# Two fp32 products made from split operands, with new engine orders and the first depthwise tap on ScalarE

## The reference, cut to what matters

```
x = x + L0(_gn(x))     # gate: sparsemax(mean(x) @ gate_w.T + gate_b); weight = sum_k gate_k * expert_w[k]; 1x1 convolution
x = x + L1(_gn(x))     # depthwise 3x3, BN, relu, prune(4.0); pointwise 256x256, BN, relu, prune(0.001)
x = x + L2(_gn(x))     # q, k, v; q2n, k2n normalised squares; kv = k2n^T v; attn = v + q2n kv / sqrt(N); @ Wln + bln
x = x + L3(_gn(x))     # 3x3 box filter
```

## Time and profile before

| what | value |
|---|---|
| times of three runs | 1614.42, 1614.85, 1618.74 us; median 1614.85 |
| the profiled execution | 1618.37 us, span 1616.7 us |
| PE busy | 1517.5 us (94%) |
| DVE busy | 1308.9 us (81%) |
| ACT busy | 1186.3 us (73%) |
| POOL busy | 295.7 us (18%) |

### The profile page before, as it was taken

How to read it: one execution, slowest core, us unless ns; L and a number is a source line. 1 busy time by engine, 2 the same in 40 slices (tenths; PEclk the granted TensorE clock), 3 DMA queues, 4 the chain that set the end, 5 groups by cost and what they waited for, 6 DMA issues and landing times.

```text
span 1616.7 us, 27652 instructions
## 1 busy us (share of the span) xinstructions
PE 1517.5 (94%) x9282; PEld 1219.5 (75%) x9282; DVE 1308.9 (81%) x2355; ACT 1186.3 (73%) x2440; POOL 295.7 (18%) x232
## 2 busy tenths in 40 slices
PE   4369999999999999999999999999999999999983
PEld 2147878788778788887877888878787887787773
DVE  4758788888888888988888889888888888887436
ACT  3356778877777887777778877777788777776752
POOL 1100022222112122221221222212222221121100
PEclk9679999999999999999999999999999999999986
DMA  4100144333344433334444333344443333344431
GB/s 133 37 20 24 38 100 91 70 83 89 89 79 99 99 75 84 79 82 97 79 99 99 66 88 85 79 82 97 99 90 69 84 87 88 60 81 80 80 61 40
DMA packets 45572, 127.88 MB, mean 79 GB/s; under 512 B 3793, under 2 KB 4817, under 8 KB 45522
## 3 DMA queue, kind: packets, MB, share of 16 engines
q0 software_dynamic: 24480, 72.26, 27.4%
q1 hardware_dynamic: 20946, 54.98, 8.9%
q10 hardware_dynamic: 96, 0.00, 0.0%
HBM read 29.29 MB, written 97.94 MB: 79 GB/s over the span
## 4 chain that ended last, share of the span: by engine, by line
PE 89%; DVE 6%; ACT 3%; issue 2%; DMA 0%; ACTq 0%; DVEq 0%
PE conv_ps L477 35%; PE tile_ps L630 12%; PE tile_ps L559 10%; PE conv_ps L618 9%; PE small_ps L605 4%; PE tile_ps L504 4%; PE tile_ps L491 3%; PE tile_ps L587 3%; PE tile_ps L526 3%; PE tile_ps L523 2%; PE tile_ps L556 2%; DVE h L823 2%; PE tile_ps L575 1%; PE small_ps L468 1%; PE small_ps L461 1%
## 5 line engine op out<-in xcount | busy, mean ns | idle before, releaser
L823 DVE SCALAR_TENSOR_TENSOR h<-xpad,dw_sb,h 128x784 f32<-128x784 f32 x512 | 492.4, 1028 | 0.0
L630 PE MATMUL tile_ps<-k,xT 112*128 112x256 f32 x896 | 201.4, 383 | 0.0
L630 PEld LDWEIGHTS tile_ps<-k,xT 112*128 112x128 f32 x896 | 171.6, 192 | 22.4
L1325 POOL TENSOR_SCALAR pw_masked<-pw_sb,hmask 128x256 f32<-128x256 f32 x64 | 117.3, 1840 | 385.7 <-DVE hmask L831 377.3
L559 PE MATMUL tile_ps<-wqk,xn_parts 128*112 128x256 f32 x1344 | 187.6, 294 | 0.0
L1315 POOL DMA_DIRECT2D out<-row_sums x90 | 108.4, 1204 | 429.4 <-DMA out<-row_sums 384.3
L1036 ACT ACTIVATE junk<-x 128x784 bf16<-128x784 f32 x192 | 162.9, 852 | 27.2 <-DVE x L850 17.9
L477 PE MATMUL conv_ps<-h,pw_masked 128*128 128x392 f32 x512 | 176.7, 499 | 5.5 <-issue 5.5
L618 PE MATMUL conv_ps<-x,mixed 128*128 128x392 f32 (+1 forms) x512 | 174.5, 493 | 2.2 <-ACT mixed L1075 1.1
L559 PEld LDWEIGHTS tile_ps<-wqk,xn_parts 128*112 128x112 f32 x1344 | 169.6, 175 | 0.1
L477 PE MATMUL conv_ps<-xn_parts,w_out 128*128 128x392 f32 x768 | 150.9, 345 | 0.0
(11 more groups left out here) (146 smaller groups left out, 2722.5 us busy)
## 6 DMA issues: line engine op xcount, KB each, us to landing
out<-row_sums POOLq DMA_DIRECT2D x90, 784.0 KB, 7.1
x<-x SPq DMA_DIRECT2D x32, 784.0 KB, 5.4
out<-x SPq DMA_DIRECT2D x30, 784.0 KB, 3.4
expert_sb<-expert_rows SPq DMA_DIRECT2D x8, 256.0 KB, 5.1
out<-x SPq DMA_DIRECT2D x4, 392.0 KB, 2.4
x<-w_qk SPq DMA_DIRECT2D x1, 512.0 KB
x<-w_vT SPq DMA_DIRECT2D x1, 256.0 KB
x<-w_ln SPq DMA_DIRECT2D x1, 256.0 KB
```

Of the source, the lines that this page charges most:

```text
L630: mm = nc.tensor.matmul(tile_ps[:, KX_BANK, i * C:(i + 1) * C], xT[:, m, half(i)], k2[:, m, :], start=(m == 0), stop=(m == M - 1))
L823: ins = nc.vector.scalar_tensor_tensor(acc, view, scalar, acc, ALU.mult, ALU.add)
L1325: nc.gpsimd.tensor_scalar(pw_masked[:, j, :], pw_sb[:, j, :], hmask[:, j:j + 1], 0.0, ALU.mult, ALU.add).then_inc(pw_masked_ready.sem, 1)
```

## The change

Both fp32 products take the form that the others have. The pointwise weight is split once in setup. The prune mask is applied to the activation, not to the weight: ACT makes the high part (`h_high`, scale = mask) and DVE the low part (`h_low`). For the mixed convolution ACT makes the high part of x0, in the instruction that also sums x0 (`x0_high`). POOL makes the low part (`x0_low`), ACT the high part of the mixed weight, and DVE its low part (`mixed_low`). POOL's `mask_weights` is gone, and ACT makes the first depthwise tap of each half. The orders on all four engines change. `h_parts` and `q_parts` share one tile.

```diff
@@ pe
             def pointwise(C_, halves):
-                pe.wait_ge(h_ready.sem, h_ready.at(C_))
-                pe.wait_ge(pw_masked_ready.sem, pw_masked_ready.at(C_))
+                pe.wait_ge(h_lo.sem, h_lo.at(C_))
...
-                    conv_tile(j, [(pw_masked[:, i, :], h[:, C_.odd, i, :]) for i in range(J)]).then_inc(pw_mm.sem, 1)
+                    conv_tile(j, by_parts(pw_parts, h_parts)).then_inc(pw_mm.sem, 1)
@@ pe, mixed_conv
-                pe.wait_ge(mixed_ready.sem, mixed_ready.at(A))
+                pe.wait_ge(mean_low.sem, mean_low.at(A))
+                pe.wait_ge(x0_lo.sem, x0_lo.at(A))
+                pe.wait_ge(mixed_lo.sem, mixed_lo.at(A))
...
+                    for n, (u, v) in enumerate(((0, 0), (0, 1), (1, 0))):
+                        for i in range(J):
+                            for a in range(2):
+                                width = HALF + 2 * a
+                                mm = nc.tensor.matmul(conv_ps[:, 2 * j + a, 0:width],
+                                                      mixed_parts[:, u, i * C + j * P:i * C + (j + 1) * P],
+                                                      x0_parts[:, v, i, a * HALF:a * HALF + width],
...
@@ pe, step
                     key_norms(E)
+                if A.active:
+                    gate_logits(A)
+                if E.active:
                     attention_weights(E)
                     value_out(B, D, E, F, 1)
-                if A.active:
-                    gate_logits(A)
@@ dve
+            def h_low(C_):
+                for j in range(J):
+                    dve.wait_ge(h_hi.sem, h_hi.at(C_, j + 1))
+                    nc.vector.scalar_tensor_tensor(h_parts[:, 1, j, :], h[:, C_.odd, j, :], hmask[:, j:j + 1],
+                                                   h_parts[:, 0, j, :].bitcast(F32), ALU.mult,
+                                                   ALU.subtract).then_inc(h_lo.sem, 1)
+            def mixed_low(A):
+                dve.wait_ge(mixed_hi.sem, mixed_hi.at(A))
...
+                    nc.vector.scalar_tensor_tensor(mixed_parts[:, 1, cols], small_ps[:, cols], gn_r[:, 0, i:i + 1],
+                                                   mixed_parts[:, 0, cols].bitcast(F32), ALU.mult,
...
@@ dve, setup
+                parts_of(pw_parts, pw_raw)
@@ dve, step
                 if E.active:
+                    q_low(E)
                     key_norms(E)
-                    q_low(E)
-                if B.active:
-                    depthwise(B, slice(0, 1))
+                if A.active:
+                    sparsemax(A)
+                    mean_lows(A)
                 if E.active:
                     attention_weights_low(E)
-                if A.active:
-                    sparsemax(A)
                 if t.first:
                     setup_weights()
                 if D.active:
                     x2_low(D)
                 if E.active:
-                    make_x3(E)
-                if B.active:
-                    depthwise(B, slice(1, 3))
+                    make_x3(E, 0)
                 if C_.active:
                     h_mask(C_)
+                if E.active:
+                    make_x3(E, 1)
...
+                if C_.active:
+                    h_low(C_)
+                if A.active:
+                    mixed_low(A)
+                if B.active:
+                    depthwise(B, slice(0, 2))      # 16 taps now: 2, then 9, then 5 (were 1, 2, 9 and 6 of 18)
@@ act
+            def x0_high(Z):
+                act.wait_ge(x_loaded.of(Z), x_loaded.at(Z))
+                if (Z - 1).active:
+                    act.wait_ge(conv0_mm.sem, conv0_mm.at(Z - 1))
+                for j in range(J):
+                    nc.scalar.activation(x0_parts[:, 0, j, 0:HW], x0[:, Z.odd, j, :], ACT.Identity,
+                                         accum_out=gn_in[:, 0, j:j + 1]).then_inc(x0_hi.sem, 1)
+            def first_tap(B, j):
...
+                nc.scalar.activation(image_rows(h[:, B.odd, j, :]), xpad[:, j, 0:H, 0:W], ACT.Identity,
+                                     scale=dw_sb[:, j, 0:1]).then_inc(dw_step[j].sem, 1)
@@ act, step
                 if D.active:
                     normalise_x2(A, D)
+                if C_.active:
+                    relu_h(C_, 0)
+                    relu_h(C_, 1)
                 if E.active:
                     attention_weights_high(E)
-                if C_.active:
-                    relu_h(C_, 0)
+                if F.active:
+                    normalise_x3(F)
                 if D.active:
                     x2_high(D)
-                if F.active:
-                    normalise_x3(F)
                 if C_.active:
                     sum_over_h(C_, 0)
-                    relu_h(C_, 1)
+                    sum_over_h(C_, 1)
+                    h_high(C_)
                 if A.active:
                     scaled_mix(A)
-                if C_.active:
-                    sum_over_h(C_, 1)
+                if B.active:
+                    for j in range(J):
+                        first_tap(B, j)
...
                     fourth_powers(D)
+                if Z.active:
+                    x0_high(Z)
@@ pool
-            def normalise_x1(A, B, C_):
+            def normalise_x1(A, B, C_, E):
                 pool.wait_ge(gn.sem, gn.at(A))
+                if E.active:
+                    pool.wait_ge(x3_ready.sem, x3_ready.at(E, 1))
...
+            def x0_low(Z):
+                for j in range(J):
+                    pool.wait_ge(x0_hi.sem, x0_hi.at(Z, j + 1))
+                    nc.gpsimd.tensor_tensor(x0_parts[:, 1, j, 0:HW], x0[:, Z.odd, j, :], x0_parts[:, 0, j, 0:HW].bitcast(F32),
+                                            ALU.subtract).then_inc(x0_lo.sem, 1)
@@ pool, step
                 if F.active and not F.in_tail:
-                    add_rows(F)
+                    add_rows(F, range(2))
+                if Z.active:
+                    x0_low(Z)
+                if F.active and not F.in_tail:
+                    add_rows(F, range(2, BOX_ROWS))
```

More of the change, by code:

```diff
@@ L163, in build @@
         h = sb("h", [P, 2, J, HW])
-        pw_masked = sb("pw_masked", [P, J, C])
         x2 = sb("x2", [P, 2, J, HW])
@@ L248, in build @@
         gn = sig("gn", GN_DONE)
-        gn_sums = [sig(f"gn_sums{n}", 2 * J if n == 0 else J) for n in range(4)]
+        gn_sums = [sig(f"gn_sums{n}", J) for n in range(4)]
         gn_mm = sig("gn_mm")
@@ L351, in build @@
         PAIRS = [[2 * b, 2 * b + 1] if 2 * b + 1 < M else [2 * b] for b in range(4)]
-        TAP_TURNS = [(j, n) for n in range(TAPS) for j in range(J)]
+        TAP_TURNS = [(j, n) for n in range(1, TAPS) for j in range(J)]
         block = ctx.enter_context(nc.Block())
@@ L842, in make_x2, with mean_lows @@
                                                    accum_out=gn_in[:, 2, j:j + 1]).then_inc(x2_ready.sem, 1)
+            def mean_lows(A):
+                dve.wait_ge(mean_column.sem, mean_column.at(A))
+                nc.vector.tensor_tensor(x0_parts[:, 1, :, HW:XW], gn_avg[:, 0, 0:2].unsqueeze(2).to_broadcast([P, J, 2]),
+                                        x0_parts[:, 0, :, HW:XW].bitcast(F32), ALU.subtract).then_inc(mean_low.sem, 1)
+            def mixed_low(A):
+                dve.wait_ge(mixed_hi.sem, mixed_hi.at(A))
+                for i in range(J):
+                    cols = slice(i * C, (i + 1) * C)
+                    nc.vector.scalar_tensor_tensor(mixed_parts[:, 1, cols], small_ps[:, cols], gn_r[:, 0, i:i + 1],
+                                                   mixed_parts[:, 0, cols].bitcast(F32), ALU.mult,
+                                                   ALU.subtract).then_inc(mixed_lo.sem, 1)
             def make_x1(A):
@@ L850, in make_x1, with make_x3 @@
                     nc.vector.scalar_tensor_tensor(split(x1[:, A.odd, j, :]), conv_banks(j), shift,
-                                                   split(x0[:, A.odd, j, 0:HW]), ALU.subtract, ALU.add,
+                                                   split(x0[:, A.odd, j, :]), ALU.subtract, ALU.add,
                                                    accum_out=gn_in[:, 1, j:j + 1]).then_inc(x1_ready.sem, 1)
-            def make_x3(E):
-                if (E - 1).active and not (E - 1).in_tail:
-                    dve.wait_ge(stored.of(E - 1), stored.at(E - 1))
-                for j in range(J):
-                    if (E - 1).active:
-                        dve.wait_ge(x3pad_ready.sem, x3pad_ready.at(E - 1, j + 1))
-                    dve.wait_ge(attn_mm.sem, attn_mm.at(E, j + 1))
-                    nc.vector.scalar_tensor_tensor(split(x3_of(E)[:, j, :]), conv_banks(j), b_out[:, j:j + 1],
-                                                   split(x2[:, E.odd, j, :]), ALU.add, ALU.add,
-                                                   accum_out=gn_in[:, 3, j:j + 1]).then_inc(x3_ready.sem, 1)
+            def make_x3(E, j):
+                if (E - 1).active:
```

(23 more changed lines are left out.)

141 lines of the change are left out of this document (73 added, 68 removed).

## The result

The changed kernel takes 1596.88 us (median of 4 runs, 1595.6 to 1599.65); the kernel before, run beside it, 1615.56. The ratio is 0.9884, 95% interval 0.9864 to 0.9904: faster, by 1.2%. The forecast was 1597. The profiled execution has a span of 1596.0 (before 1616.7), 20.7 less.

The account below looks back on a forecast made before the run. PE was taken as the bound, busy 46.44 of 46.44 us a full round. 28 full rounds x (46.45 - 45.5) = 26.6, less 7.2 for filling and draining, is 19.4 saved: 1597 us, 8-in-10 range 1577 to 1624.

Parts of the forecast that it names:

- round 0: Filling: mixed product waits for DVE's mixed_low behind the longer setup; round closes at 49.2 instead of 39.6, +9.6 us.
- round 1: Filling: all taps wait behind the mixed weight on DVE, +4.8 us.
- round 2: Filling: the pointwise product starts earlier, no longer waiting for POOL and taps, -4.8 us.
- The front: Start of a full round: relus on ACT and sparsemax on DVE precede attention's parts; ACT makes PE wait 0.9 us.
- The products: PE's pointwise and mixed products in split form save 0.97 and 0.89; PE's work falls from 46.44 to 44.58 a round.
- The new form is not cheaper here: Rival: split products save little, for instance through the 394 columns; a round of 46.2, 1615 us, chance 0.03.
- DVE's round: DVE's work, waits and POOL's blocks: 41.5 + 1.7 = 43.2 occupied; with remaining waits 45.5, equal to PE's.
- the thin place: DVE's round equals PE's 45.5, so each us of DVE lateness costs about half a us a round.
- Filling and draining: First rounds and drain together cost +7.2 us, with bounds of +2 and +14.
- Everything hides: Rival: ACT's high part comes sooner, PE keeps 1.6 or more of its 1.86; round 44.8, 1576 us, chance 0.12.
- The lock bites harder: Rival: POOL's x0_low or xpad blocks DVE more, DVE 1.2 later; round 46.1, 1612 us, chance 0.18.
- DVE becomes the bound: Rival: x0_low or its blocks make DVE late, PE waits 1.9; round 46.5, 1625 us, slower, chance 0.17.

Follow-up runs that it names:

- the doubled low part: Changed kernel, but GpSimd makes the low part of x0 twice in every half, two more instructions a round: 1718.42 us, ratio 1.0622.
- the kernel with three moves: Changed kernel with attention's high part ahead of relu_h, its low part ahead of sparsemax, first taps behind the second square_k: 1585.02 us, ratio 0.9801.
- all of it: Changed kernel with those three moves of instructions plus round 0's mixed_low ahead of the weight setup: 1578.14 us, ratio 0.9757.
- the early mixed_low alone: Changed kernel with only round 0's mixed_low moved ahead of the pointwise weight setup on VectorE: 1590.98 us, ratio 0.9833.
- the high parts alone: Changed kernel, mixed product multiplies only the high parts, 16 of its 24 records left out: 1567.3 us, ratio 0.9693.

## Why the prediction was right

The forecast of 1597 came from a sum of -19.4 against the profiled execution's -20.7, and by the mechanism named. That it meets 1596.88 so closely is luck: it was taken between 1595.5 and 1599, by which median or execution one starts from, and the terms of filling and draining are off by up to 3.7.

| step | forecast | measured |
|---|---|---|
| PE's own work in a full round | 44.58 | 44.73 |
| new wait before attention_out | 0.92 | 0.73 and 0.82 in turn |
| who sets it | ACT's relus, DVE ready 0.6 earlier | ACT; DVE waits 0.70 and 0.62 |
| a full round | 45.5 | 45.50 |
| 28 full rounds | -26.6 | -27.8 |
| round 0 | +9.6 | +10.4 |
| round 1 | +4.8 | +5.1 |
| round 2 | -4.8 | -1.8 |
| round 3 | -1.8 | -2.4 |
| drain | -0.6 | -4.3 |

*The front.* This step held by experiment, not only by the row. Of its two edits, the relus' move takes the wait away and sparsemax's doesn't touch it.

*The products.* Their price was read from products of the same form, and each costs 4.54. The old price, 5.45, comes back when they go back to one pass, and so does the expected loss: with the products undone the rest of the change is 1.0 a round slower than before. "The new form is not cheaper here" falls.

*DVE's round.* Its sum was too high in the places where two engines meet, and the error did not reach the time, because PE and ACT set it. x0_low, unknown before, takes 1.70 each (I took 1.75). The Trainium skill, GPSIMD Engine Reference, section "3.1 Elementwise — side-by-side cycle accounting", gave an estimate of 1.7, and the trace agrees. Its block on the taps was 0.4 (5.22 less 4.81), not 0.9, and that of xpad on the row sums 0.7 (2.47 less 1.79), not 0.8. DVE's waits for ACT add up to 3.2 in a full round, where the forecast left 2.3. I called DVE "the thin place", from which each us costs half a us. That slope was mis-sized: 1.1 us of DVE work more (the first tap) cost a round nothing, 3.4 more cost 4.0. The 1.1 vanished because 0.45 of it filled the wait for y's sums and 0.4 came back from x0_low's block, so gate_in was at most 0.2 later. gate_in had some room (ready at 842.14, taken at 842.52), and a pause of PE there replaces the later one of 0.77. So about 1 us of lateness at gate_in costs nothing, an estimate from these rows; the doubled low part lies beyond that, where most of each us counted, and PE's slower clock added 2.1. That DVE idles for ACT further on (1.90 in the kernel with three moves) doesn't help gate_in.

*Filling and draining.* The sum, +7.2 against +7.1, is right by two misses that nearly cancel. Round 2 gained 3.0 less, since two x0_low fell on DVE's y work there. DVE's timeline of round 2 has an instruction of 0.17 at 1.81 and one of 1.03 at 2.30:

```profile
103.57 1.81 DVE L848 TENSOR_SCALAR ymask<-y_over 128x2 f32<-128x2 f32 x1
105.42 2.30 DVE L852 SCALAR_TENSOR_TENSOR x<-x,ymask 128x784 f32<-128x784 f32 x1
```

Leaving x0_low out gave 2.9 of it back. The drain gained 3.7 more than I gave it. I had put nothing there for its cheaper products. With the products undone the drain takes 166.5, so they are 1.5 of it; the rest stays open.

*The rivals.* "Everything hides" asked for tighter relus, but ACT's chain was as tight as counted and the wait stayed. "The lock bites harder" didn't come about, since both places cost less. "DVE becomes the bound" was real and at most one GpSimd pair away, as the doubled low part shows.

*What was left on the table.* PE's own 44.7 would be a round without waits. Each wait taken away uncovered a smaller one: the attention's low part 0.77, a bank behind square_k 0.5, gate_in 0.4. From 45.50 three moves of instructions came to 45.07.

## What to carry to other kernels

Where an operation of one engine's queue is moved ahead of another, time the chain on both engines that feed the same waiting instruction and name the later one; only moving that one pays. A round at its limit can have a second limit close behind (here 0.77 became 0.5, then 0.4), so give the gain of a removed wait only down to the next. Before adding a GpSimd instruction, look at what VectorE runs at that moment: beside instructions with an operand in PSUM it was free (scale_q takes 1.84 with and without it), beside two-input ones in SBUF each that got in cost 1.45 of its 1.7.

## What the runs showed of the hardware

Who pays when GpSimd and VectorE want the shared port is not fixed by the instructions. Beside a stream of 16 taps the same two x0_low took 11.13 (changed kernel), 9.87 (all of it) or 13.42 us (first tap on VectorE), with the taps at 15.22, 15.22 and 15.21; each time GpSimd ended 3.2 us after the last tap. With the early mixed_low alone they took 4.56, and with the high parts alone 4.97, the taps both times at 18.12. In full rounds of the doubled low part GpSimd got in each time, with 8.18 for five taps instead of 4.81. Alone a pair takes 3.37 to 3.39. How far into the stream GpSimd asked does not decide it: it had to wait when it asked 5.0, 7.3 and 8.6 us after the first tap, and got in at 3.8 and 6.1. What does decide it stays open. The Trainium skill, SBUF — State Buffer, section "Who interferes with whom", says that issue order, not the shape of the operation, decides who blocks. The trace agrees as to the shape, and adds that a waiting GpSimd instruction need not get its turn when the running tap ends: it stood through up to ten taps.

PE's clock was at 1.00 in full rounds with pauses of up to 1.5 us, but for two neighbouring rounds of the kernel with the high parts alone: after pauses of 1.45 and 1.36 it read 0.66 (870 to 875) and 0.67 (914.87 to 920), and the rounds lasted 1.0 longer. After the doubled low part's pauses of 2.73 and 2.56 it read 0.50 (867.59 to 871.00) and 0.61 (917.60 to 922.00). Every full round of that kernel has a mean of 0.93 or 0.97, which added 2.1 us a round to the pause itself. Why pauses of this shorter kind were followed by a lower clock twice and otherwise not is not shown.
